# Inverse transforms moved ahead of v's first chunk, four patch-row buffers, and more groups of the 1x1 layer early

## The chip, the cores and the metric

The kernel runs on one core of a Trainium2 chip. The metric is the device time of one execution in microseconds (us). Three runs of the kernel before gave 2798.39, 2808.57 and 2824.54 us, the median being 2808.57 us.

## The reference

The input is x of shape (16, 32, 128, 128) in fp32. Two blocks follow each other, each added to its input:

```python
    x = x + _L0_conv_ref(_gn(x), ...)      # gated depthwise 3x3 with mixed kernels, then 1x1
    x = x + _L1_conv_ref(_gn(x), ...)
```

`_gn` has one channel per group, so it normalises every channel of an image by its own mean and variance. The change lies in the second block, which is

```python
        hidden = jnp.einsum('oc,bchw->bohw', w_hidden, x)          # 32 -> 192 channels
        hidden = lax.conv_general_dilated(hidden, w_dw, ...)       # depthwise 3x3
        q, k, v = jnp.split(hidden, 3, axis=1)                     # 64 channels each
        q_fft = jnp.fft.rfft2(to_patch(q).astype(jnp.float32))     # patches of 8x8
        k_fft = jnp.fft.rfft2(to_patch(k).astype(jnp.float32))
        out = jnp.fft.irfft2(q_fft * k_fft, s=(p, p))
        ...
        mu = out.mean(axis=1, keepdims=True)                       # over the 64 channels
        var = out.var(axis=1, keepdims=True)
        out_norm = (out - mu) / jnp.sqrt(var + 1e-05)
        out_norm = out_norm * norm_w[None, :, None, None] + norm_b[None, :, None, None]
        gated = v * out_norm
        return jnp.einsum('oc,bchw->bohw', w_out, gated)
```

## The kernel before, in words

Stage one (to about 520 us) runs the first block image by image and stores the normalised result to memory with a zero border. Stage two (from about 560 us) runs the second block in 32 **units**, each half an image (64 rows of 128 pixels). Every engine has a written-out list of instructions; semaphores alone tie them together, and each engine runs its list strictly in order. A unit has two parts on every engine.

- **front(u, half, tail)** interleaves two things. For unit u, the 1x1 layer of q and k: VectorE copies a row of patches with their border (`window`, line 1099) into one of the `win` buffers, four groups of matmuls read each (`hidden_group`, line 558; 32 groups in a unit), and ScalarE copies each group's result out of one of three PSUM banks (`windows_out`, line 811). For the unit before (`tail` = u - 1), its end: VectorE takes statistics over the channels of the inverse transform Y (`pixel_stats`, line 1109, and `variance`, lines 1115 and 1117), GpSimd raises them to -1/2 (`roots`, line 441), VectorE centres and scales Y in eight pieces (lines 1122 and 1129), TensorE transposes a piece (`turn`, line 590), ScalarE copies it to `gated` (`turned_out`, line 820), VectorE multiplies it by v (`gate`, line 1134), and TensorE projects two pieces at a time (`project`, line 599); `residual` (line 1141) adds the input. v itself is a dense 3x3 convolution in eight chunks (`v_chunk`, line 577, 18 matmuls each), into three PSUM banks in turn; from chunk 3 on a chunk waits for the gate two chunks back. Groups of the 1x1 layer are spread inside the chunks by a table.
- **spectral(u, ...)** does the transforms of unit u: q's (`q_octet`, line 637) and k's (`k_quad`, line 654, sixteen of them), VectorE's sixteen products of both (line 1199) into the `prod` buffers, and the inverse (`inverse_octet`, line 670, eight of them), whose results ScalarE copies to Y in pairs (`inverse_out`, line 865; `s_y_ready`). The list ends with v's chunk 0 of unit u and, behind it, inverse octets 6 and 7. The statistics of the next front wait for both copies of that last pair.

A gate stands in VectorE's list ahead of the patch-row copy of its turn, and waits for ScalarE's copy of the transposed piece. A patch-row copy waits until the groups that read its buffer last are done. The first two patch rows of a unit are copied in the spectral part before.

## Time and profile before

| what | us |
|---|---|
| median of 3 runs | 2808.57 (2798.39 to 2824.54) |
| the profiled execution, its own time | 2816.34 |
| its span, first to last instruction | 2814.5 |
| TensorE busy | 2513.6 (89%) |
| VectorE busy | 1650.5 (59%) |
| ScalarE busy | 1440.8 (51%) |
| GpSimd busy | 471.8 (17%) |
| TensorE's mean granted clock | 0.965 of full speed |

Busy shares are averages over both stages. The timeline of an engine lists merged runs of instructions with their start, their length and, in brackets, the idle time before them with what ended it. The table of waits sums such idle times by the line that waited and the line that released it. Ends of matmuls are modelled, so the start of the next instruction is the safer mark on TensorE. In the profile fp32 matmuls are recorded twice (16 instructions of line 670 stand as x32).

### The profile page before, as it was taken

Reading aid. Unit: us, or ns where it says so; the run is one execution under the profiler, and the core shown is the slowest. Engines: PE = TensorE matmul, PEld = TensorE weight load, DVE = VectorE, ACT = ScalarE, POOL = GpSimd, SP = SyncE. Lnnn points to the kernel's source line nnn. Section 1 sums busy time; section 2 is a strip of 40 time slices with the busy share of each in tenths; the row PEclk is TensorE's granted clock in tenths of the full one; section 3 lists DMA queues with packets and bytes.
Section 4 is the critical chain, followed back from the end, with each engine's and each line's share of the span. In section 5 each row is a group of like instructions: output and inputs, shape, how many; then the busy total and the mean of one; then the engine's idle time right before and its main releaser. Section 6 shows DMA issues by size and latency. Waiting matters only on the chain.

```text
span 2814.5 us, 90655 instructions
## 1 busy us (share of the span) xinstructions
PE 2513.6 (89%) x40199; PEld 1659.2 (59%) x40199; DVE 1650.5 (59%) x4058; ACT 1440.8 (51%) x2381; POOL 471.8 (17%) x322
## 2 busy tenths in 40 slices
PE   7888889789999999999999899998999989999998
PEld 3333333466666666666666666666666666666665
DVE  4656666455555555555555556555555555656555
ACT  3545555645455555555555455555555555555552
POOL 1000000021111212112121112122212122212221
PEclk9988988899999999999999999999999999999999
DMA  6788887622222222222222222222222222222221
GB/s 128 184 214 202 213 227 203 165 66 62 57 63 59 63 63 67 63 59 67 59 67 63 59 63 63 63 65 61 67 63 66 61 62 66 68 60 67 63 52 46
DMA packets 60345, 248.30 MB, mean 88 GB/s; under 512 B 12393, under 2 KB 12658, under 8 KB 53714
## 3 DMA queue, kind: packets, MB, share of 16 engines
q1 hardware_dynamic: 59954, 242.50, 35.3%
q8 instruction: 317, 5.19, 0.8%
q14 instruction: 74, 0.61, 0.1%
HBM read 140.74 MB, written 101.72 MB: 86 GB/s over the span
## 4 chain that ended last, share of the span: by engine, by line
PE 58%; DVE 14%; ACT 5%; issue 3%; SPq 0%; DMA 0%; DVEq 0%
PE bank L654 16%; PE bank L577 11%; PE bank L670 9%; PE bank L637 7%; PE bank L590 6%; PE bank L558 5%; ACT arena L820 4%; PE bank L599 4%; DVE arena L1109 3%; DVE arena L1122 3%; DVE arena L1134 2%; DVE arena L1129 2%; DVE arena L1099 2%; DVE arena L1141 2%; ACT arena L865 1%
## 5 line engine op out<-in xcount | busy, mean ns | idle before, releaser
L441 POOL TENSOR_TENSOR arena<-arena 128x8 f32<-128x8 f32 x256 | 447.6, 1748 | 1814.8 <-DVE arena L1115 1809.8
L577 PE MATMUL bank<-arena 128*64 128x512 f16 x4608 | 713.4, 403 | 5.5 <-ACT arena L865 5.5
L811 ACT ACTIVATE arena<-bank 100x512 f32<-100x512 f32 x1024 | 615.7, 630 | 183.8 <-PE bank L558 166.7
L1199 DVE TENSOR_TENSOR arena<-bank,arena 128x512 f32<-128x512 f32 x512 | 354.1, 692 | 457.4 <-PE bank L654 370.6
L558 PEld LDWEIGHTS bank<-arena 128*36 128x36 f16 (+1 forms) x8192 | 332.0, 106 | 382.5 <-DVE arena L1099 157.8
L654 PE MATMUL bank<-arena 100*64 100x128 f32 x8192 | 513.1, 274 | 15.4 <-issue 8.7
L558 PE MATMUL bank<-arena 128*36 128x128 f16 (+1 forms) x8192 | 406.1, 224 | 122.1 <-DVE arena L1099 115.8
L654 PEld LDWEIGHTS bank<-arena 100*64 100x64 f32 x8192 | 457.5, 136 | 54.4 <-issue 47.3
L512 PE MATMUL bank<-arena 32*32 32x508 f32 (+1 forms) x9216 | 389.7, 660 | 57.7 <-issue 42.9
L820 ACT ACTIVATE arena<-bank,arena 128x256 f32<-128x256 f32 x512 | 261.1, 560 | 191.6 <-PE bank L590 189.6
L865 ACT ACTIVATE arena<-bank 128x512 f32<-128x512 f32 x256 | 139.1, 596 | 406.1 <-PE bank L670 406.1
L1134 DVE TENSOR_TENSOR arena<-arena,bank 128x512 f32<-128x512 f32 x256 | 176.0, 687 | 270.1 <-ACT arena L820 268.7
L857 ACT ACTIVATE arena<-bank 128x512 f32<-128x512 f32 x256 | 149.2, 598 | 338.6 <-PE bank L637 325.2
L1109 DVE BATCH_NORM_STATS2 arena<-arena 128x6 f32<-128x128 f32 x1024 | 221.9, 279 | 139.2 <-ACT arena L865 139.2
L637 PE MATMUL bank<-arena 100*64 100x128 f32 x4096 | 274.3, 275 | 4.7 <-ACT arena L857 3.2
L512 PEld LDWEIGHTS bank<-arena 32*32 32x32 f32 x9216 | 142.7, 108 | 207.2 <-issue 177.2
L577 PEld LDWEIGHTS bank<-arena 128*64 128x64 f16 x4608 | 211.2, 112 | 87.8 <-ACT arena L865 11.0
L670 PE MATMUL bank<-arena 64*64 64x256 f32 x4096 | 254.8, 383 | 1.3 <-issue 1.3
L637 PEld LDWEIGHTS bank<-arena 100*64 100x64 f32 x4096 | 233.2, 137 | 30.6 <-issue 17.9
L590 PE MATMUL bank<-arena 128*128 128x128 f32 x1024 | 181.9, 301 | 66.6 <-DVE arena L1129 59.9
L590 PEld LDWEIGHTS bank<-arena 128*128 128x128 f32 x1024 | 133.8, 195 | 167.2 <-DVE arena L1129 101.2
L670 PEld LDWEIGHTS bank<-arena 64*64 64x64 f32 x4096 | 143.6, 131 | 84.4 <-issue 32.7
(112 smaller groups left out, 1620.6 us busy)
## 6 DMA issues: line engine op xcount, KB each, us to landing
arena<-xn_d SPq DMA_DIRECT2D x128, 536.2 KB, 8.3
xn_d<-arena SPq DMA_DIRECT2D x130, 260.0 KB, 4.5
x_d<-arena SPq DMA_DIRECT2D x64, 512.0 KB, 8.3
arena<-x_d SPq DMA_DIRECT2D x128, 256.0 KB, 4.9
out<-arena SPq DMA_DIRECT2D x128, 256.0 KB, 5.3
arena<-x_in SPq DMA_DIRECT2D x32, 544.0 KB, 10.1
arena<-x_in SPq DMA_DIRECT2D x32, 528.0 KB, 10.0
arena<-spectra_in SPq DMA_DIRECT2D x1, 1152.0 KB
```

The lines of the kernel that those rows point to most:

```text
L441: pool.tensor_tensor(tiny["rstd"][:, slot], tiny["var_eps"][:, slot], powers, ALU.pow).then_inc(s_root, 1)
L512: mm = pe.matmul(at(psum_of(t, r)[32 * c:32 * c + 32, :], low, [W, 4], [1, high - low]), conv_w[b % 2][32 * r:32 * r + 32, 32 * tap:32 * t ...
L558: mm = pe.matmul(banks[g % ring][low:high, 128 * i:128 * i + 128], w[:, first + low:first + high], hidden_w, start=True, stop=True)
L577: mm = pe.matmul(v_banks[chunk % 3][64 * s:64 * s + 64, :], v_w[:, 64 * tap:64 * tap + 64], at(xs[half], row * WP + 32 * k + dx, [32 * WP, ...
L590: tr = pe.transpose(t_bank[:, 128 * i:128 * i + 128], at(Y, 8 * k + 4 * jr + i, [32, 128]), ident)
L637: mm = pe.matmul(banks[m % 2][64 * par:64 * par + 64, 128 * pair:128 * pair + 128], G_q[0:WIN, 64 * ch:64 * ch + 64], hwin[0:WIN, 128 * ch ...
L654: mm = pe.matmul(k_banks[n % 3][64 * par:64 * par + 64, 256 * part + 128 * pair:256 * part + 128 * pair + 128], G_k[0:WIN, 128 * ch + 64 * ...
L670: mm = pe.matmul(i_banks[par][64 * lam:64 * lam + 64, 256 * (m % 2):256 * (m % 2) + 256], small["inverse"][64 * par:64 * par + 64, 64 * pa ...
L811: act.activation(h_rows[0:WIN, :, first:first + 4], banks[g % ring][0:WIN, :].rearrange("p (i c) -> p c i", i=4), ACT.Copy).then_inc(s_h_r ...
L820: ins = act.activation(at(gated[jr], 256 * lam, [32, 8], [8, 4], [1, 8]), at(banks[4], 64 * lam, [8, 8], [128, 4], [1, 8]), ACT.Identity, ...
L1109: ins = dve.bn_stats(T["pixel_stats"][:, first:first + 6], at(Y, 2048 * s + 4 * p + j, [32, 64], [1, 2]))
L1199: dve.tensor_tensor(parts(prod[m % 4][:, 512 * second:512 * second + 512]), parts(k_banks[n % 3]), q_sb[m % 2][:, 256 * second:256 * secon ...
```

## The change

- **TensorE.** Inverse octets 6 and 7 of a unit now stand ahead of v's chunk 0 instead of behind it. The wait for the last products, which stood ahead of the chunk's last tap, is now ahead of octet 7. Three groups of the 1x1 layer instead of two stand ahead of chunk 1, five instead of four are inside it, and the chunks after it hold 5, 5, 4, 4, 3, 3 instead of 5, 5, 5, 4, 4, 3. ScalarE's list follows (8, 5, 5, 4, 4, 3, 3 groups ahead of the transposed pieces instead of 6, 5, 5, 5, 4, 4, 3).
- **VectorE.** There are four `win` buffers instead of two, so four patch rows instead of two are copied in the spectral part before; the other four come one before the loop over pieces, and three in it, ahead of the gate instead of behind it.
- **Memory.** The `prod` buffers go from four to three to make room.

The first place is **TensorE's list at the seam between two units**: the last k_quads (line 654, 652 in the changed file), v's chunks (577, 575), the inverse (670, 668) and the groups of the 1x1 layer (558). Before:

```order
L670 MATMUL bank<-arena 64x256 x16
L654 MATMUL bank<-arena 64x128 x24
L577 MATMUL bank<-arena 64x512 x18
L670 MATMUL bank<-arena 64x256 x16
L558 MATMUL bank<-arena 64x128
L558 MATMUL bank<-arena 36x128
L558 MATMUL bank<-arena 64x128
...
L558 MATMUL bank<-arena 64x128
L558 MATMUL bank<-arena 36x128
L577 MATMUL bank<-arena 64x512 x6
L558 MATMUL bank<-arena 64x128
L558 MATMUL bank<-arena 36x128
```

The same place now:

```order
L668 MATMUL bank<-arena 64x256 x16
L652 MATMUL bank<-arena 64x128 x24
L668 MATMUL bank<-arena 64x256 x16
L575 MATMUL bank<-arena 64x512 x18
L558 MATMUL bank<-arena 64x128
L558 MATMUL bank<-arena 36x128
L558 MATMUL bank<-arena 64x128
...
L558 MATMUL bank<-arena 64x128
L558 MATMUL bank<-arena 36x128
L575 MATMUL bank<-arena 64x512 x4
L558 MATMUL bank<-arena 64x128
L558 MATMUL bank<-arena 36x128
```

The inverse pair (x16) and chunk 0 (x18) have changed places. The rows left out are groups of the 1x1 layer alone, eight rows a group: two groups before, three now, and then one more inside chunk 1, after its first six matmuls before and after its first four now.

The second place is **VectorE's list from the ninth product of a unit to the second scale of the front**: products (line 1199, 1198 in the changed file), patch-row copies (1099, 1100), centre (1122, 1123) and scale (1129, 1130). Before:

```order
L1199 TENSOR_TENSOR arena<-bank,arena 128x512 x7
L1099 COPY arena<-arena 128x1600
L1199 TENSOR_TENSOR arena<-bank,arena 128x512 x3
L1099 COPY arena<-arena 128x1600
L1199 TENSOR_TENSOR arena<-bank,arena 128x512 x4
...
L1129 TENSOR_TENSOR arena<-arena 128x128x4
L1099 COPY arena<-arena 128x1600
L1122 TENSOR_TENSOR arena<-arena 128x128x4
L1129 TENSOR_TENSOR arena<-arena 128x128x4
L1099 COPY arena<-arena 128x1600
```

The same place now:

```order
L1198 TENSOR_TENSOR arena<-bank,arena 128x512 x7
L1100 COPY arena<-arena 128x1600
L1198 TENSOR_TENSOR arena<-bank,arena 128x512 x2
L1100 COPY arena<-arena 128x1600
L1198 TENSOR_TENSOR arena<-bank,arena 128x512
L1100 COPY arena<-arena 128x1600
L1198 TENSOR_TENSOR arena<-bank,arena 128x512 x2
L1100 COPY arena<-arena 128x1600
L1198 TENSOR_TENSOR arena<-bank,arena 128x512 x2
...
L1130 TENSOR_TENSOR arena<-arena 128x128x4
L1123 TENSOR_TENSOR arena<-arena 128x128x4
L1130 TENSOR_TENSOR arena<-arena 128x128x4
L1100 COPY arena<-arena 128x1600
```

Two more patch-row copies stand among the products, and the copy between the first scale and the second centre is gone.

The third place is **VectorE's list in the front, where the second and third gates stand** (gate 1134, 1135 in the changed file; statistics 1109, 1115, 1117, now 1110, 1116, 1118). Before:

```order
L1109 BN_STATS arena<-arena 128x6 x4
L1115 TENSOR_SCALAR arena<-arena 128x8
L1117 COPY arena<-arena 128x8
L1134 TENSOR_TENSOR arena<-arena,bank 128x512
L1122 TENSOR_TENSOR arena<-arena 128x128x4
L1129 TENSOR_TENSOR arena<-arena 128x128x4
L1099 COPY arena<-arena 128x1600
L1109 BN_STATS arena<-arena 128x6 x4
```

The same place now:

```order
L1110 BN_STATS arena<-arena 128x6 x4
L1116 TENSOR_SCALAR arena<-arena 128x8
L1118 COPY arena<-arena 128x8
L1100 COPY arena<-arena 128x1600
L1135 TENSOR_TENSOR arena<-arena,bank 128x512
L1123 TENSOR_TENSOR arena<-arena 128x128x4
L1130 TENSOR_TENSOR arena<-arena 128x128x4
L1110 BN_STATS arena<-arena 128x6 x4
```

The copy stood behind the gate, centre and scale, and stands ahead of the gate.

The diff:

```diff
--- before.py
+++ after.py
@@ -265,7 +265,7 @@
         hwin = take(128 * 128)
         Y = take(64 * 64)
         q_sb = [take(512) for _ in range(2)]
-        prod = [take(1024) for _ in range(4)]
+        prod = [take(1024) for _ in range(3)]
         gated = [take(512) for _ in range(2)]
         res = take(2048)
         xs_1, xs_0 = [take(HALF * WP, f16) for _ in range(2)]
@@ -273,7 +273,7 @@
         assert stage1_end <= top[0] - (HALF * WP + 1) // 2
         G_q = take(64 * 64)
         G_k = take(64 * 128)
-        win = [take(1632, f16) for _ in range(2)]
+        win = [take(1632, f16) for _ in range(4)]
 
 
         block = ctx.enter_context(nc.Block())
@@ -416,11 +416,11 @@
             pool.wait_ge(s_prep_v, 1)
             pool.memset(xh.bitcast(f32), 0.0).then_inc(s_pads_zero, 1)
             pool.memset(xl.bitcast(f32), 0.0).then_inc(s_pads_zero, 1)
-            for s in range(2):
+            for s in range(4):
                 pool.memset(win[s][:, 16 * WIN:1632].bitcast(f32), 0.0).then_inc(s_win_room, 1)
             pool.wait_ge(s_pool_consts, 2)
             pool.wait_ge(s_pads_zero, 2)
-            pool.wait_ge(s_win_room, 2)
+            pool.wait_ge(s_win_room, 4)
 
             for b in range(-1, NB + 1):
                 pool.wait_ge(s_ve, b + 2)
@@ -551,7 +551,7 @@
                     pe.wait_ge(s_x2_ready, NCH * NB)
                 if positive(32 * u + g + 1 - ring):
                     pe.wait_ge(s_h_ready, 32 * u + g + 1 - ring)
-                w = win[g // 4 % 2]
+                w = win[g // 4 % 4]
                 for i in range(4):
                     first = (4 * (g % 4) + i) * WIN
                     for low, high in ((0, 64), (64, WIN)):
@@ -559,7 +559,7 @@
                                        start=True, stop=True)
                 mm.then_inc(s_hidden_mm, 1)
 
-            def v_chunk(u, half, k, jr, groups, between, before_last=None):
+            def v_chunk(u, half, k, jr, groups, between):
 
                 chunk = 2 * k + jr
                 if chunk == 0:
@@ -569,8 +569,6 @@
                 if chunk > 2:
                     pe.wait_ge(s_gated, 8 * u + chunk - 2)
                 for tap in range(9):
-                    if tap == 8 and before_last is not None:
-                        before_last()
                     dy, dx = tap // 3, tap % 3
                     for s in range(2):
                         row = 8 * (2 * s + jr) + dy
@@ -615,14 +613,14 @@
                     hidden(16)
                     return
                 v_half = 1 - half
-                hidden(2)
+                hidden(3)
                 for k in range(4):
-                    v_chunk(tail, v_half, k, 1, (4, 5, 4, 3)[k], hidden)
+                    v_chunk(tail, v_half, k, 1, (5, 5, 4, 3)[k], hidden)
                     if k > 0:
                         project(tail, k - 1)
                     turn(tail, k, 0)
                     if k < 3:
-                        v_chunk(tail, v_half, k + 1, 0, (5, 5, 4)[k], hidden)
+                        v_chunk(tail, v_half, k + 1, 0, (5, 4, 3)[k], hidden)
                     if k < 3 or u is None:
                         turn(tail, k, 1)
 
@@ -669,7 +667,7 @@
                             for lam in range(2):
                                 mm = pe.matmul(i_banks[par][64 * lam:64 * lam + 64, 256 * (m % 2):256 * (m % 2) + 256],
                                                small["inverse"][64 * par:64 * par + 64, 64 * part:64 * part + 64],
-                                               at(prod[m % 4][64 * par:64 * par + 64, :], 256 * part + 64 * lam, [512, 2], [128, 2], [1, 64]),
+                                               at(prod[m % 3][64 * par:64 * par + 64, :], 256 * part + 64 * lam, [512, 2], [128, 2], [1, 64]),
                                                start=part == 0, stop=part == 1)
                     mm.then_inc(s_inverse_mm, 1)
 
@@ -689,9 +687,12 @@
                     k_quad(2 * m + 1)
                     if m == 0 and tail is not None:
                         project(tail, 3)
-                v_chunk(u, half, 0, 0, 0, None, lambda: inverse_inputs(7))
+                pe.wait_ge(s_prod_ready, 16 * u + 14)
+                pe.wait_ge(s_y_ready, 8 * u + 6)
                 inverse_octet(6)
+                pe.wait_ge(s_prod_ready, 16 * u + 16)
                 inverse_octet(7)
+                v_chunk(u, half, 0, 0, 0, None)
 
             front(0, 0, None)
             spectral(0, 0, None)
@@ -841,7 +842,7 @@
                     high(NB - 1, 1)
                     act.wait_ge(s_xl_ready, 4 * NB)
                     return
-                for p, groups_before in enumerate((6, 5, 5, 5, 4, 4, 3)):
+                for p, groups_before in enumerate((8, 5, 5, 4, 4, 3, 3)):
                     some(groups_before)
                     turned_out(tail, p // 2, p % 2)
                 if u is None:
@@ -1092,11 +1093,11 @@
 
             def window(u, half, r, b=None):
 
-                if positive(32 * u + 4 * (r - 1)):
-                    dve.wait_ge(s_hidden_mm, 32 * u + 4 * (r - 1))
+                if positive(32 * u + 4 * (r - 3)):
+                    dve.wait_ge(s_hidden_mm, 32 * u + 4 * (r - 3))
                 if r == 0:
                     dve.wait_ge(s_xs_in[half], 64 * (b + 1))
-                dve.tensor_copy(win[r % 2][:, 0:16 * WIN].rearrange("p (j y x) -> p j y x", y=10, x=10),
+                dve.tensor_copy(win[r % 4][:, 0:16 * WIN].rearrange("p (j y x) -> p j y x", y=10, x=10),
                                      at(xs[half], 8 * r * WP, [8, 16], [WP, 10], [1, 10])).then_inc(s_win_ready, 1)
 
             def pixel_stats(u, p):
@@ -1141,7 +1142,7 @@
                 dve.tensor_tensor(piece, banks[6].rearrange("p (l r w) -> p l r w", l=2, r=8), piece, ALU.add).then_inc(s_res_done, 1)
 
             def front(u, half, tail):
-                rows = iter(range(2, 8) if u is not None else ())
+                rows = iter(range(4, 8) if u is not None else ())
 
                 def windows(n=1):
                     for r in islice(rows, n):
@@ -1150,7 +1151,6 @@
                 if tail is None:
                     second_stats(NB - 1, range(4, NCH))
                     aggregate(NB + 2, NB - 1, None)
-                    windows(2)
                     quarter_variance(NB + 2, None)
                     low(NB - 2, 0)
                     low(NB - 2, 1)
@@ -1168,7 +1168,6 @@
                     if p == 1:
                         centre(tail, 0)
                 scale(tail, 0)
-                windows()
                 centre(tail, 1)
                 scale(tail, 1)
                 windows()
@@ -1176,6 +1175,8 @@
                     if p < 5:
                         pixel_stats(tail, p + 3)
                         variance(tail, p + 3)
+                    if p > 0:
+                        windows()
                     if p < 7 or u is None:
                         gate(tail, p // 2, p % 2)
                     if p < 6:
@@ -1183,8 +1184,6 @@
                         scale(tail, p + 2)
                     if p in (2, 4, 6):
                         residual(tail, p // 2 - 1)
-                    if p > 0:
-                        windows()
 
             def spectral(u, tail, nxt):
                 if tail is not None:
@@ -1193,20 +1192,20 @@
                     m, second = n // 2, n % 2
                     dve.wait_ge(s_q_copied, 8 * u + m + 1)
                     dve.wait_ge(s_k_mm, 16 * u + n + 1)
-                    if positive(8 * u + m - 3):
-                        dve.wait_ge(s_inverse_mm, 8 * u + m - 3)
+                    if positive(8 * u + m - 2):
+                        dve.wait_ge(s_inverse_mm, 8 * u + m - 2)
                     parts = lambda a: a.rearrange("p (part x) -> p part x", part=2)
-                    dve.tensor_tensor(parts(prod[m % 4][:, 512 * second:512 * second + 512]), parts(k_banks[n % 3]),
+                    dve.tensor_tensor(parts(prod[m % 3][:, 512 * second:512 * second + 512]), parts(k_banks[n % 3]),
                                       q_sb[m % 2][:, 256 * second:256 * second + 256].unsqueeze(1).broadcast_to([128, 2, 256]),
                                       ALU.mult).then_inc(s_prod_ready, 1)
                     if n == 1 and tail is not None:
                         residual(tail, 3)
-                    if nxt is not None and n in (8, 11):
-                        window(nxt[0], nxt[1], (n - 8) // 3, nxt[2])
-
-            dve.wait_ge(s_win_room, 2)
-            window(0, 0, 0, 0)
-            window(0, 0, 1, 0)
+                    if nxt is not None and n in (8, 10, 11, 13):
+                        window(nxt[0], nxt[1], (8, 10, 11, 13).index(n), nxt[2])
+
+            dve.wait_ge(s_win_room, 4)
+            for r in range(4):
+                window(0, 0, r, 0)
             front(0, 0, None)
             dve.wait_ge(s_xn_out, 128 * NB)
             spectral(0, None, (1, 1, 0))
```

## Rows read from the trace of the kernel before

**Rows 1.** The page, the chain that ended last: share of the span by engine.

```profile
PE 58%; DVE 14%; ACT 5%; issue 3%; SPq 0%; DMA 0%; DVEq 0%
```

**Rows 2.** Waits of TensorE, 590 to 2790 us: total us, times, longest us.

```profile
PE bank L558 <- DVE arena L1099: 111.5, 93, 1.6
PE bank L590 <- DVE arena L1129: 59.9, 32, 2.7
PE bank L654 <- issue: 8.7, 6, 1.8
```

**Rows 3.** Timeline of TensorE, one unit: start us, length us, instructions, idle before.

```profile
1015.01 2.23 PE L577 MATMUL bank<-arena 128*64 128x512 f16 x18
1017.17 1.98 PE L670 MATMUL bank<-arena 64*64 64x256 f32 x32
1019.08 0.64 PE L558 MATMUL bank<-arena 128*64 128x128 f16 x16
...
1024.86 0.71 PE L590 MATMUL bank<-arena 128*128 128x128 f32 x4 [1.85 <-DVE arena L1129]
...
1031.04 0.65 PE L577 MATMUL bank<-arena 128*64 128x512 f16 x4
...
1034.23 1.02 PE L599 MATMUL bank<-arena 128*64 128x512 f32 x4
...
1038.59 0.39 PE L577 MATMUL bank<-arena 128*64 128x512 f16 x2
1040.22 0.41 PE L558 MATMUL bank<-arena 128*64 128x128 f16 x8 [1.25 <-DVE arena L1099]
```

**Rows 4.** Timeline of VectorE, same unit, same columns.

```profile
1015.28 0.69 DVE L1199 TENSOR_TENSOR arena<-bank,arena 128x512 f32<-128x512 f32 x1 [0.18 <-PE bank L654]
1020.34 0.88 DVE L1109 BATCH_NORM_STATS2 arena<-arena 128x6 f32<-128x128 f32 x4 [4.36 <-ACT arena L865]
...
1024.11 0.69 DVE L1129 TENSOR_TENSOR arena<-arena 128x512 f32<-128x512 f32 x1
...
1031.57 0.87 DVE L1109 BATCH_NORM_STATS2 arena<-arena 128x6 f32<-128x128 f32 x4
...
1032.62 0.68 DVE L1134 TENSOR_TENSOR arena<-arena,bank 128x512 f32<-128x512 f32 x1
1033.22 0.69 DVE L1122 TENSOR_TENSOR arena<-arena 128x512 f32<-128x512 f32 x1
1034.01 0.69 DVE L1129 TENSOR_TENSOR arena<-arena 128x512 f32<-128x512 f32 x1
1034.62 0.57 DVE L1099 COPY arena<-arena 128x1600 f16<-128x1600 f16 x1
```

**Rows 5.** Timeline of ScalarE, same unit.

```profile
1019.22 1.09 ACT L865 ACTIVATE arena<-bank 128x512 f32<-128x512 f32 x2 [5.65 <-PE bank L670]
...
1025.61 1.02 ACT L820 ACTIVATE arena<-bank,arena 128x256 f32<-128x256 f32 x2 [1.94 <-PE bank L590]
...
1032.06 3.05 ACT L811 ACTIVATE arena<-bank 100x512 f32<-100x512 f32 x5
```

**Rows 6.** Timeline of GpSimd, same unit.

```profile
1021.57 5.82 POOL L441 TENSOR_TENSOR arena<-arena 128x8 f32<-128x8 f32 x3 [44.48 <-DVE arena L1115]
1029.73 1.64 POOL L441 TENSOR_TENSOR arena<-arena 128x8 f32<-128x8 f32 x1 [2.35 <-DVE arena L1115]
```

**Rows 7.** Timeline of TensorE: v's chunk 0 (units 0, 30, 31), last first transpose.

```profile
591.14 2.23 PE L577 MATMUL bank<-arena 128*64 128x512 f16 x18
...
2700.25 2.23 PE L577 MATMUL bank<-arena 128*64 128x512 f16 x18
...
2769.27 2.24 PE L577 MATMUL bank<-arena 128*64 128x512 f16 x18
...
2779.12 0.71 PE L590 MATMUL bank<-arena 128*128 128x128 f32 x4 [2.73 <-DVE arena L1129]
```

**Rows 8.** Stretches: us, busy PE, PEld, DVE, ACT, POOL, granted clock, DMA share, GB/s.

```profile
1025.50:1029.60 4.10, 4.10 (x41) 2.53 (x42) 2.62 (x10) 2.55 (x5) 1.88 (x1) 0.58 0.01 4
```

## The prediction

> **What bounds the kernel now.** I read the chain of waits by engine first: 58% of the span is TensorE, 14% VectorE, 5% ScalarE [rows 1]. So the question is where TensorE stands still. The table of TensorE's waits answers it for stage two: 111.5 us in groups of the 1x1 layer that wait for a patch-row copy, 59.9 us in transposes that wait for VectorE's scale, and 8.7 us in k_quads that wait for nothing the profile shows [rows 2]. Then I laid the timelines of one unit side by side and measured on TensorE from start to start.
>
> Times from here on are in us after the first matmul of v's chunk 0, which stands at 1015.01 [rows 3]. *Before*: chunk 0 runs 0 to 2.16, the inverse pair 2.16 to 4.07, and then the groups begin [rows 3]. ScalarE's two Y copies start 2.05 after the pair does and last 1.09; VectorE starts its statistics at 5.33 and ends the first scale 4.46 later, at 9.79 [rows 4, 5]; the first transpose starts at 9.85 [rows 3]. TensorE has by then run two groups and a chunk with four. A chunk alone is 2.16 and a chunk with five groups 3.19 (1031.04 to 1034.23), so a group is some 0.21 [rows 3]. Its work ends near 4.07 + 0.42 + 3.04 = 7.6. It stands for about 2.2, of which the profile books 1.85 at the transpose and the rest, with modelled ends, elsewhere.
>
> The group waits have one pattern. The gate stands ahead of the patch-row copy in VectorE's list, the gate waits for ScalarE's copy of a transposed piece, and the next groups wait for the patch row. Such a stall is longer than it is booked: at 1038.59 two matmuls of a chunk start, worth 0.24, and the group behind them starts at 1040.22, so 1.39 against 1.25 [rows 3].
>
> **The change, part by part.**
>
> *Inverse ahead of chunk 0.* Octet 6 needs products that are long done. Octet 7 needs the product of the sixteenth k_quad: 0.27 to 0.96 [rows 4]. Octet 6 takes half of the pair's 1.91 us and ends at 0.96. With 0.06 from VectorE's end to TensorE's start (first scale to transpose, 1024.80 to 1024.86 [rows 3, 4]) octet 7 starts at 1.05: a new stall of 0.1. The pair ends at 2.0, ScalarE copies from 2.15 to 3.24, statistics start at 3.27, and the first scale ends at 7.73, so the transpose may start at 7.8. The same copies of Y are now hidden behind chunk 0.
>
> *TensorE up to there.* 2.0, chunk 0 to 4.2, three groups to 4.8, chunk 1 with five groups to 8.0 or 8.1. Work ends after the data are there: no stall, 0.3 to spare. Three banks take the groups' results. ScalarE needs 0.61 a group (3.05 for five [rows 5]), and its first starts about 4.7, so the fourth group (5.3) meets a bank that comes free at 5.3. Inside a chunk a group comes every 0.7, slower than ScalarE. Cost here: 0 to 0.2, taken as nothing.
>
> The transpose starts at 8.1 instead of 9.85 with two more groups done: 1.75 + 0.42 = **2.2 us a unit**.
>
> *Four patch-row buffers, copies ahead of the gates.* VectorE's spacing in the front is 1.05 for statistics, 0.60 gate, 0.79 centre, 0.61 scale, about 0.5 copy [rows 4]. Carried on from 7.73: second scale to 9.1, the fifth patch row to 9.6, statistics to 10.6, first gate 10.6 to 11.3, the sixth row at 14.2, the seventh at 17.8, the eighth at 22.9. TensorE, without a stall, wants these rows at 15.3, 19.8, 23.6 and 28. Each is there 5 us early, so none of the three stalls is left: 111.5 / 31 = 3.6 a unit booked, and 0.15 more for each of three, **4.0 us a unit**.
>
> *What is late next.* The gates. TensorE's own walk has transposes at 8.1, 12.0, 16.9, 20.6, 25.1, 28.6 and 33.0. From a transpose ScalarE starts after 0.75 and takes 1.02 [rows 3, 5], then the gate 0.69. Chunk 3 starts at 12.7 and wants the first gate (11.3). The projections start at 15.9, 24.2 and 32.0 and want the second, fourth and sixth gate (14.95, 23.6, 31.2). Nothing is late, the least margin is 0.6.
>
> *Two more copies among the products.* The one behind the fourteenth product holds back the fifteenth by 0.2 and ends before the sixteenth can start; the one behind the eleventh holds back the twelfth by 0.2, which TensorE wants 0.4 later still. Three `prod` buffers: each product waits for an inverse three octets back, and that stands ahead of the k_quad it needs in TensorE's list. Both cost nothing; if their cover were gone they cost 0.2 to 0.5 a unit. The start of stage two waits for memory, and is as before.
>
> *The clock.* In the stretch behind the 1.85 us idle time TensorE's granted clock is 0.58 on average, mostly the lower level of 1.2 GHz [rows 8]. Not all units have it. The last unit's period is 69.02 (2700.25 to 2769.27), the mean of 31 is (2769.27 - 591.14) / 31 = 70.26 [rows 7]. So 31 x 1.24 = 38.4 us lie above the undisturbed unit; 8.7 are the waits for nothing [rows 2], **29.7** I put on the clock. What came before the fall was a TensorE that stood still. With the stall gone I expect all of it back; bounds 0 and 29.7, and I take the upper one, since in no other place of the unit does it fall.
>
> For the waits for nothing the Trainium skill has "Runtime: NRT & Kernel Launch", section "Instruction fetch mechanics": instructions are fetched in blocks while the engine runs on, and crossing a block is "mostly hidden". If these waits are fetches, the trace disagrees in six places of up to 1.8 us [rows 2]; by that rule they would be nearly gone and the time 8.7 lower. I leave them where they are.
>
> *The end.* Behind the last unit there are no groups. Its first transpose waits for the same chain: 9.85 now (2769.27 to 2779.12 [rows 7]), 7.8 after: **2.1**.
>
> Sum: 31 x (2.2 + 4.0) = 192, and 29.7, and 2.1: 224 us. From the profiled execution's own 2816.3 that is **2592 us**. The median of the runs shown is 0.3% lower, at 2808.6; I hold that the runs differ mostly in how many units have the low clock, which is gone afterwards, so I leave it at 2592.
>
> **The rivals.**
>
> *The clock falls all the same.* For it: the small matmuls of the groups are more crowded near the first transpose, and I have only one cause by timing. Price: 29.7 back, 2622. Chance 13%.
>
> *The first transpose waits, or the gates do, for GpSimd.* It needs 5.82 for its first three roots where one alone takes 1.64 [rows 6], and the second root ends just when the second scale wants it (8.4). VectorE is now denser there. If the second scale comes up to 1.4 later, so do the first two gates, and the first projection waits up to 0.3 to 1: 10 to 31 us, 2602 to 2623. Against it: a single root beside three tensor operations of VectorE still took 1.64. Chance 8%. The Trainium skill speaks for this rival in "SBUF — State Buffer": VectorE and GpSimd share a port pair as an exclusive lock that an instruction holds to its end. The first three roots (1.94 each) agree in direction, the single one does not show it.
>
> *The copies are not what the groups wait for.* Then ScalarE's banks would be, at once, and the 4.0 would shrink to half: 2654. Against it: no wait of a group for ScalarE stands in the table. Chance 4%.
>
> *A denser TensorE is granted less clock through the whole front.* This is the one that ends slower. Price: work at 0.58 takes 1.72 times as long, so once 9 us of each front's 33 run low, the 6.2 gained are lost; were it half of a front, 31 x (12 - 6.2) = +180, 2996. Against it: the spectral part is dense now and no part of it is known to fall; a clock that falls behind busy time was not seen. Chance 2%. Some 2% more are for the change not coming to effect, 2800.
>
> **How the numbers follow.** My forecast has 71%. It holds from 2575 (8.7 of the waits go, and some noise: the runs before spread by 0.9%) to 2610 (0.1 to 0.5 a unit in small stalls at the banks). The range reaches to the clock and GpSimd rivals: 2572 to 2640. Two executions of this kernel cannot be told apart by much less than 1%. Faster by over 1%: 0.95; within 1%: 0.02; slower by over 1%: 0.03.
>
> **What would show it.** The waits of a group for a patch row near 0 instead of 111.5; the wait of the transpose for the scale near 0; a wait of octet 7 for a product of about 0.1 a unit; a unit's period near 62.8; a granted clock near 1 in every front. The forecast is wrong if the transpose still waits over 0.5 a unit, if groups wait for ScalarE's copies, or if the low clock stays with no idle time ahead of it.

## The result and the profile after

The changed kernel takes 2586.6 us (median of 4 runs, 2583.2 to 2590.4) against 2807.2 us before (4 runs); the ratio is 0.921, 95% interval 0.916 to 0.925. The forecast was 2592 us, from 2572 to 2640. The profiled execution took 2588.67 us with a span of 2586.9, against 2816.34 and 2814.5.

The chain of waits of the changed kernel, by engine, answers to [rows 1]. In the profile after, line numbers are shifted: 575 is v's chunk, 588 the transpose, 597 the projection, 635 q, 652 k, 668 the inverse, 812 and 821 ScalarE's copies, 866 its Y copies, 1100 the patch rows, 1110 the statistics, 1130 the scale, 1135 the gate, 1142 the residual, 1198 the products.

```profile
PE 76%; issue 1%; ACT 1%; DVE 0%; SPq 0%; DMA 0%; ACTq 0%
```

VectorE's 14% are gone from it, and TensorE is busy 95% of the span. The waits of TensorE in stage two, 560 to 2560 us (total, times, longest), answer to [rows 2]:

```profile
PE bank L652 <- issue: 7.0, 6, 1.6
PE bank L652 <- DVE arena L1198: 6.7, 1, 6.7
PE bank L588 <- ACT arena L821: 5.5, 31, 0.2
PE bank L588 <- DVE arena L1130: 1.5, 1, 1.5
```

The 111.5 us of groups that waited for a patch row have no row any more. Of the transposes' 59.9 us one wait of 1.5 is left, in the last front, which has no groups. The 6.7 stand once, at the start of stage two. One unit on TensorE (start, length, instructions), for [rows 3]; the point zero of the prediction, the end of the last k_quad, is now the start of the inverse pair:

```profile
966.38 2.84 PE L652 MATMUL bank<-arena 100*64 100x128 f32 x48
969.15 2.02 PE L668 MATMUL bank<-arena 64*64 64x256 f32 x32
971.11 2.25 PE L575 MATMUL bank<-arena 128*64 128x512 f16 x18
973.20 0.83 PE L558 MATMUL bank<-arena 128*64 128x128 f16 x24
...
977.14 0.71 PE L588 MATMUL bank<-arena 128*128 128x128 f32 x4
...
1002.64 1.10 PE L635 MATMUL bank<-arena 100*64 100x128 f32 x16
```

The pair takes 1.96 from start to start (1.91 in [rows 3]), so octet 7's wait for its product costs 0.05. The first transpose comes 7.99 after the last k_quad instead of 9.85, with two more groups done, and no row of the front has an idle time in brackets. VectorE and ScalarE at the same seam, for [rows 4, 5]; first VectorE:

```profile
968.19 0.57 DVE L1100 COPY arena<-arena 128x1600 f16<-128x1600 f16 x1
968.67 1.35 DVE L1198 TENSOR_TENSOR arena<-bank,arena 128x512 f32<-128x512 f32 x2
972.36 0.87 DVE L1110 BATCH_NORM_STATS2 arena<-arena 128x6 f32<-128x128 f32 x4 [2.34 <-ACT arena L866]
...
976.14 0.69 DVE L1130 TENSOR_TENSOR arena<-arena 128x512 f32<-128x512 f32 x1
...
982.76 0.57 DVE L1100 COPY arena<-arena 128x1600 f16<-128x1600 f16 x1
983.25 0.68 DVE L1135 TENSOR_TENSOR arena<-arena,bank 128x512 f32<-128x512 f32 x1
```

ScalarE's Y copies:

```profile
971.24 1.08 ACT L866 ACTIVATE arena<-bank 128x512 f32<-128x512 f32 x2 [3.64 <-PE bank L668]
```

The new patch-row copy at 968.19 sits in front of the last two products and they follow it back to back; they end at 970.02, 0.87 after the last k_quad (0.96 before). The Y copies start 2.09 after it, the statistics 3.21, the first scale ends at 7.68. The copy at 982.76 now stands ahead of the gate at 983.25, which finds its data.

The inverse pair of units 0, 30 and 31, and the last front's first transpose, for [rows 7]:

```profile
589.86 2.02 PE L668 MATMUL bank<-arena 64*64 64x256 f32 x32
...
2482.86 2.02 PE L668 MATMUL bank<-arena 64*64 64x256 f32 x32
...
2545.50 2.02 PE L668 MATMUL bank<-arena 64*64 64x256 f32 x32
...
2553.23 0.71 PE L588 MATMUL bank<-arena 128*128 128x128 f32 x4 [1.46 <-DVE arena L1130]
```

An undisturbed unit now lasts 62.64 (69.02 before) and the mean of 31 is (2545.50 - 589.86) / 31 = 63.09 (70.26 before). An undisturbed unit is the shortest kind, with no wait for nothing and a full clock. In these terms the 227.6 us between the two spans are 31 x 6.38 = 197.8 in the undisturbed unit, 24.7 in what disturbs units (38.5 before, 13.8 now), 1.3 before the first of them and 3.8 behind the last. The granted clock over a whole front (columns as in [rows 8]) is full:

```profile
964.40:1002.60 38.20, 38.20 (x556) 23.97 (x552) 28.70 (x81) 27.07 (x49) 14.16 (x8) 1.00 0.04 8
```

### The profile page after: what moved, and what is told of

The parts are those of the page before. It is cut to its first block, busy times and chain, and to the rows that moved or that the text cites. A ratio compares the mean times of both kernels' runs of the same rounds, so it can differ in the third digit from the quotient of the medians.

```text
span 2586.9 us, 90657 instructions
## 1 busy us (share of the span) xinstructions
PE 2465.4 (95%) x40199; PEld 1644.8 (64%) x40199; DVE 1638.6 (63%) x4058; ACT 1432.4 (55%) x2381; POOL 476.5 (18%) x324
## 3 DMA queue, kind: packets, MB, share of 16 engines
q1 hardware_dynamic: 59954, 242.50, 38.5%
## 4 chain that ended last, share of the span: by engine, by line
PE 76%; issue 1%; ACT 1%; DVE 0%; SPq 0%; DMA 0%; ACTq 0%
PE bank L575 21%; PE bank L652 18%; PE bank L668 10%; PE bank L558 9%; PE bank L635 8%; PE bank L588 6%; PE bank L597 4%; ACT arena L821 1%; SPq L318 0%; DMA xn_d<-arena 0%; DVE arena L1110 0%; DVE arena L961 0%; ACT arena L866 0%; DVE arena L1198 0%; DVE arena L1135 0%
## 5 line engine op out<-in xcount | busy, mean ns | idle before, releaser
L575 PE MATMUL bank<-arena 128*64 128x512 f16 x4608 | 689.3, 393 | 0.0
L812 ACT ACTIVATE arena<-bank 100x512 f32<-100x512 f32 x1024 | 604.2, 628 | 95.8 <-PE bank L558 74.4
L558 PE MATMUL bank<-arena 128*36 128x128 f16 (+1 forms) x8192 | 388.9, 220 | 11.0 <-DVE arena L1100 4.2
L575 PEld LDWEIGHTS bank<-arena 128*64 128x64 f16 x4608 | 205.6, 109 | 96.3 <-issue 12.4
L1130 DVE TENSOR_TENSOR arena<-arena 128x512 f32<-128x512 f32 x256 | 178.3, 696 | 23.4
```

The source lines that it names most:

```text
L558: mm = pe.matmul(banks[g % ring][low:high, 128 * i:128 * i + 128], w[:, first + low:first + high], hidden_w, start=True, stop=True)
L575: mm = pe.matmul(v_banks[chunk % 3][64 * s:64 * s + 64, :], v_w[:, 64 * tap:64 * tap + 64], at(xs[half], row * WP + 32 * k + dx, [32 * WP, ...
L812: act.activation(h_rows[0:WIN, :, first:first + 4], banks[g % ring][0:WIN, :].rearrange("p (i c) -> p c i", i=4), ACT.Copy).then_inc(s_h_r ...
```

## The experiments

Ratios are against the kernel before, on the same chip. "Booked" is idle time as a profile writes it. Sums of waits are over all of stage two, from the first unit's end of the k_quads to the last front, unless another stretch is named.

### The two halves apart

**Patch rows alone** (four buffers, four copies in the spectral part, copies ahead of the gates):

```diff
-        win = [take(1632, f16) for _ in range(2)]
+        win = [take(1632, f16) for _ in range(4)]
...
-        prod = [take(1024) for _ in range(4)]
+        prod = [take(1024) for _ in range(3)]
...
-                    if nxt is not None and n in (8, 11):
+                    if nxt is not None and n in (8, 10, 11, 13):
...
+                    if p > 0:
+                        windows()
                     if p < 7 or u is None:
                         gate(tail, p // 2, p % 2)
...
-                    if p > 0:
-                        windows()
```

> The kernel before with the four patch-row buffers, the four copies in the spectral part and the copies ahead of the gates alone; inverse pair, group tables as before. Theory (two separate stalls, and a clock that falls behind the transpose's stall): the three group stalls go, 31 x 4.0 = 124 us, the transpose still waits about 1.8 us booked in every unit and the low clock stays in about half of the units: about 2683 us. Rival (the clock falls because of the group stalls): the low clock goes too, about 2655. Rival (the groups really wait for ScalarE's banks): half of the gain, about 2745.

Measured: 2662 us, ratio 0.950 (0.946 to 0.953). The waits of TensorE:

```profile
PE bank L590 <- DVE arena L1129: 59.9, 32, 2.7
PE bank L654 <- issue: 8.4, 6, 1.8
```

The group stalls are gone and the transpose's stall is untouched, as the theory has it, but the time is 21 us under it, near the rival's. An undisturbed unit is 64.86, so the group stalls were 4.16 a unit (69.02 before). I took a unit as low in clock where its period less its booked idle time lies over 1 us above the least of its kernel, in the units from one end of the k_quads to the next, the first of 31 left out: 15 of 30 before, 4 of 30 here. The granted clock over a unit picks out the same ones: 0.97 to 0.98 in these, 1.00 in the others. So most of the low clock went although the stall that stands ahead of it stayed.

**Inverse pair ahead of chunk 0, and the new group tables:**

```diff
-                hidden(2)
+                hidden(3)
...
-                    v_chunk(tail, v_half, k, 1, (4, 5, 4, 3)[k], hidden)
+                    v_chunk(tail, v_half, k, 1, (5, 5, 4, 3)[k], hidden)
...
-                        v_chunk(tail, v_half, k + 1, 0, (5, 5, 4)[k], hidden)
+                        v_chunk(tail, v_half, k + 1, 0, (5, 4, 3)[k], hidden)
...
-                v_chunk(u, half, 0, 0, 0, None, lambda: inverse_inputs(7))
+                pe.wait_ge(s_prod_ready, 16 * u + 14)
+                pe.wait_ge(s_y_ready, 8 * u + 6)
                 inverse_octet(6)
+                pe.wait_ge(s_prod_ready, 16 * u + 16)
                 inverse_octet(7)
+                v_chunk(u, half, 0, 0, 0, None)
...
-                for p, groups_before in enumerate((6, 5, 5, 5, 4, 4, 3)):
+                for p, groups_before in enumerate((8, 5, 5, 4, 4, 3, 3)):
```

> The kernel before with the inverse pair ahead of chunk 0 and the new group tables; two patch-row buffers, copies behind the gates. Theory: the transpose's stall goes (31 x 2.2 + 2 = 70 us) and with it the low clock (25 to 30): about 2710 us, the three group stalls as before, 3.6 us a unit. Rival (clock tied to the group stalls): 2737 with the low clock still in half of the units. Rival (the two parts need each other, since groups that come earlier wait longer for their patch rows): the group stalls grow by what the transpose gives, under 20 us gained.

Measured: 2845 us, ratio 1.014 (1.011 to 1.018): slower than before. Of the three only the last mechanism is near, and it is worse than I had it: the group waits are 200.9 us, in 124 waits of up to 2.5. No unit waits for the scale at the transpose any more (the one wait left, 1.4, is in the last front), and yet 20 of 30 are low in clock. So the transpose's stall is not needed for the low clock. The next two runs take the slowdown apart.

**Inverse pair alone** (of that diff the lines around the two octets):

> The kernel before with the inverse pair ahead of chunk 0 alone. Theory: the transpose can start 2.05 us earlier (7.8 after the point where the last k_quad ends) and TensorE's work ends at 7.65, so the booked wait falls from 1.85 to under 0.3: 31 x 2.0 + 2 = 64 us, and the low clock 25 to 30: about 2716 us. Rival (the groups ahead are what covers the chain): the wait stays over 0.5 a unit and the time over 2740.

Measured: 2721 us, ratio 0.971 (0.966 to 0.975). As expected: no wait for the scale is left in the units, group waits are 112.2 us (93 waits, as before), and no unit of 30 is low in clock.

**Group tables alone** (the other lines; 3 groups, then 5, 5, 5, 4, 4, 3, 3):

> The kernel before with the new group tables alone (3, then 5, 5, 5, 4, 4, 3, 3). Theory: the transpose starts when its data are there, 9.85 us after the last k_quad, whatever TensorE does before it; two groups of 0.21 us fill the wait: 31 x 0.4 = 13 us, booked wait about 1.4 instead of 1.85, perhaps some of the low clock: 2780 to 2794. Rival (more work ahead is as good as an earlier inverse): over 40 us gained.

Measured: 2911 us, ratio 1.039 (1.035 to 1.043). Both expectations fall. The waits of TensorE, with the same columns:

```profile
PE bank L558 <- DVE arena L1099: 207.6, 123, 2.5
PE bank L590 <- DVE arena L1129: 36.2, 32, 2.7
PE bank L558 <- ACT arena L811: 11.1, 31, 0.4
```

The transposes wait 23.7 us less: 1.08 booked in a unit instead of 1.85, of which the two groups fill 0.4 and another 0.35 is now booked at ScalarE's banks. But the groups wait 96 us more, four times in an undisturbed unit (1.72, 2.15, 1.56, 1.70) instead of three. And 21 of 30 units are low in clock. On TensorE one of these stalls:

```profile
1060.56 0.71 PE L590 MATMUL bank<-arena 128*128 128x128 f32 x4
...
1062.82 0.62 PE L577 MATMUL bank<-arena 128*64 128x512 f16 x4
1065.59 0.41 PE L558 MATMUL bank<-arena 128*64 128x128 f16 x8 [2.15 <-DVE arena L1099]
```

and on VectorE at the same time:

```profile
1062.36 0.69 DVE L1134 TENSOR_TENSOR arena<-arena,bank 128x512 f32<-128x512 f32 x1 [2.45 <-ACT arena L820]
1062.97 0.69 DVE L1122 TENSOR_TENSOR arena<-arena 128x512 f32<-128x512 f32 x1
1063.76 0.69 DVE L1129 TENSOR_TENSOR arena<-arena 128x512 f32<-128x512 f32 x1
1064.37 0.68 DVE L1141 TENSOR_TENSOR arena<-bank,arena 128x512 f32<-128x512 f32 x1
1064.97 0.57 DVE L1099 COPY arena<-arena 128x1600 f16<-128x1600 f16 x1
```

The transpose at 1060.56 has to go through ScalarE and the gate before VectorE comes to the patch row. With the old table the first group of that row stood far enough behind the transpose; one or two groups earlier in the list it stands right behind it, and the whole way of 4.4 us from transpose to patch row is on TensorE's path, less what a part of a chunk covers. Behind this stall the granted clock falls too (1066 to 1070):

```profile
1066.00:1070.00 4.00, 4.00 (x35) 2.32 (x32) 1.34 (x6) 2.38 (x5) 1.64 (x1) 0.57 0.00 0
```

### Place or number of buffers

**Copies ahead of the gates alone**, two buffers, old tables, pair behind chunk 0:

```diff
+                    if p > 0:
+                        windows()
                     if p < 7 or u is None:
                         gate(tail, p // 2, p % 2)
...
-                    if p > 0:
-                        windows()
```

> The kernel before with the copies ahead of the gates alone: two buffers, old tables, inverse pair behind chunk 0. Theory: the copy that waits behind gate, centre and scale comes 2 us earlier and no longer behind ScalarE's copy, so the three group stalls go without any more buffer: about 2662 us, as the kernel with four buffers and copies ahead of the gates. Rival (two buffers hold the copy back, because it waits for the groups that read the buffer): less than half of that, over 2740.

Measured: 2681 us (2663 to 2681; the profile is of the 2663), ratio 0.953 (0.949 to 0.957), beside 0.950 for the run with four buffers: intervals that overlap. The group waits are gone (the transposes' 60.0 us stay). Moving the two lines gives nearly all of the group term without a buffer, but not quite: an undisturbed unit is 65.18, 0.32 more than with four buffers. It stands at the first projection, which lasts 1.35 us (1248.66) instead of 1.02, since its second half waits for the second gate; ahead of that gate VectorE has one patch-row copy more to do in the front, and waits 0.40 for its buffer (1242.71 to 1243.11). The profile books none of this on TensorE.

**New tables and copies ahead of the gates**, two buffers, pair behind chunk 0:

> The kernel before with the new group tables and the copies ahead of the gates: two buffers, inverse pair behind chunk 0. The new tables alone cost 104 us, with group stalls of 1.7 and 2.2 us. Theory (the tables ask for the fourth and fifth patch rows one gate earlier, and only a copy that stands behind that gate is late): ahead of the gates the stalls go, and the tables fill part of the transpose's wait: 2645 to 2665 us. Rival (two buffers are too few for the new tables): group stalls of 1 us or more in every unit, over 2700.

Measured: 2649 us, ratio 0.944 (0.941 to 0.946). This is as the theory has it. The same tables that cost 104 us with the copies behind the gates gain some 24 with the copies ahead (31 x 0.79: an undisturbed unit is 64.39, against 65.18 in the run before this one). The waits of groups for patch rows are gone, the transposes of the units wait 33.4 us in all, and 11.1 us are waits for ScalarE's banks, 0.4 each.

**The changed kernel with the copies behind the gates**, four buffers:

```diff
-                    if p > 0:
-                        windows()
                     if p < 7 or u is None:
                         gate(tail, p // 2, p % 2)
...
+                    if p > 0:
+                        windows()
```

> The changed kernel with the patch-row copies of the front behind the gates, as they stood before (four buffers stay). Theory: with four buffers the copies have 1.6 to 3.4 us to spare even behind the gates (sixth row ready at 16.4 for 19.8, seventh at 22.0 for 23.6, eighth at 25.5 for 28), so nothing waits: 2587 us, as the changed kernel. Rival (the place ahead of the gate is what counts): group waits come back, some 1 us a unit, 2620.

Measured: 2585 us, ratio 0.921 (0.917 to 0.924). No difference, and no group wait.

**The changed kernel with two patch-row buffers** (and four product buffers), copies ahead of the gates:

> The changed kernel with two patch-row buffers and four product buffers: inverse pair ahead of chunk 0, new tables, copies ahead of the gates. Theory (order alone is enough): rows 4 to 7 ready at 14.7, 18.3, 22.4, 26.5 for groups that want them at 15.3, 19.8, 23.6, 28: 2587 to 2600 us. Rival (with the new tables the groups run ahead of two buffers, as in the runs with the tables alone, whatever stands ahead of the gate): 1 us a unit or more, over 2620.

Measured: 2588 us, ratio 0.922 (0.919 to 0.925). No difference either: an undisturbed unit is 62.63 us in all three. Buffers and place are two cures for one stall, and in this kernel either is enough.

**The changed kernel with the old group tables:**

> The changed kernel with the group tables of before (2, then 4, 5, 5, 5, 4, 4, 3). Theory: TensorE has the same work and its transpose waits 0.15 us at most: 2587 to 2592 us, so the tables are worth nothing where the inverse pair stands ahead. Rival (the tables cover the chain): a wait of 0.4 us or more in every unit, over 2600.

Measured: 2599 us, ratio 0.926 (0.922 to 0.929); an undisturbed unit is 62.83. This lies between the two expectations, so neither is right in size. TensorE's rows there:

```profile
971.07 2.02 PE L668 MATMUL bank<-arena 64*64 64x256 f32 x32
...
978.29 0.39 PE L558 MATMUL bank<-arena 128*64 128x128 f16 x8
978.80 0.71 PE L588 MATMUL bank<-arena 128*128 128x128 f32 x4
```

The transpose stands 7.73 behind the last k_quad, 0.05 after the scale has ended (978.75), and 0.51 behind the last group, where it stands 0.32 behind it when nothing is awaited (976.82 to 977.14 in the changed kernel). The stall of 0.2 is hidden in a matmul's modelled end and booked as nothing; 31 of them are 6 us of the 12.

### The clock, and the start of stage two

**A long stall at the transpose and nowhere else.** The changed kernel, the first scale held back until GpSimd's third root:

```diff
+                dve.wait_ge(s_root, 8 * tail + 3)
                 scale(tail, 0)
                 centre(tail, 1)
```

> The changed kernel with the first scale of each front held back until GpSimd's third root is done, 2.8 us later than in the changed kernel, so that TensorE waits some 2.4 us (booked 2.2) at the first transpose of every unit and nowhere else. Theory (the low clock needs the transpose's stall together with the group stalls, since with either alone it was nearly gone): 31 x 2.4 = 74 us more, the clock stays high in nearly all units: 2655 to 2670 us. Rival (a single stall of over 2 us is enough for the clock): low clock in half of the units or more, 1.6 us each, 2685 to 2720.

Measured: 2682 us, ratio 0.957 (0.954 to 0.959), with booked waits of 2.2 in every unit. The time lies between theory and rival, and the clock is low in 7 of 30 units (the first one, left out, is an eighth). In one of them the fall stands right behind the stall (1190 to 1194 us):

```profile
1190.00:1194.00 4.00, 3.78 (x30) 2.38 (x32) 3.86 (x12) 1.64 (x3) 0.81 (x1) 0.57 0.02 4
```

In the run with the patch rows alone, one of the four low units has it elsewhere, behind a wait for nothing of 1.56 us in the spectral part (836 to 840 us):

```profile
836.00:840.00 4.00, 3.57 (x34) 1.92 (x33) 0.69 (x1) 0.00 (x0) 0.00 (x0) 0.62 0.38 151
```

The other three of that run have it behind the transpose's 1.85, and six of the seven of the other behind the transpose's 2.2. So a stall of 1.5 to 2.2 us can be followed by the low clock without any group stall, and mostly is not: "both stalls together" is refuted as a condition. Nine of these eleven low units also had a wait for nothing of 0.6 to 1.7 us, two of them right ahead of the fall, the others 28 to 31 us ahead of it. But of the 15 low units of the kernel before only four had one, so that is no condition either.

The low clock does not need a stall that the change removes. The changed kernel with the copies behind the gates has it in one unit of 30, right behind a wait for nothing:

```profile
1770.34 0.45 PE L652 MATMUL bank<-arena 100*64 100x128 f32 x4 [1.88 <-issue]
...
1770.00:1774.00 4.00, 3.66 (x36) 2.02 (x36) 0.69 (x1) 0.00 (x0) 0.00 (x0) 0.58 0.37 140
```

The next run below has it in two of 30, behind such waits of 1.6 and 2.0 us. What decides between one unit and the next stays open.

**No wait for the stores at the start of stage two:**

```diff
-            dve.wait_ge(s_xn_out, 128 * NB)
             spectral(0, None, (1, 1, 0))
```

> The changed kernel without VectorE's wait, ahead of the first product of stage two, for all stores of the normalised images. With three product buffers those buffers no longer share memory with the tile that is being stored; the wait is for nothing. In the changed kernel TensorE stands 6.7 us in the third k_quad there and VectorE 10.3 us for the stores. Theory: the products begin some 9 us earlier, the ninth product's patch-row copy then waits some 2 us for its load, 6 to 9 us gained: 2578 to 2581 us. Rival (the load of the next half's rows, which waits for the same stores, sets the pace): the wait moves there, under 2 us gained.

**The changed kernel again, on the same chip:**

> The changed kernel as it is, beside the next one on the same chip. Theory and rival alike: 2587 us, from 2580 to 2592.

Measured: 2586.8 us without the wait (0.922, 0.920 to 0.925), 2585.7 with it (0.922, 0.920 to 0.924): nothing gained, the rival. VectorE's rows there:

```profile
570.84 0.69 DVE L1198 TENSOR_TENSOR arena<-bank,arena 128x512 f32<-128x512 f32 x1 [1.05 <-PE bank L652]
578.43 0.58 DVE L1100 COPY arena<-arena 128x1600 f16<-128x1600 f16 x1 [6.90 <-DMA arena<-xn_d]
```

VectorE gets through nine products, and then the patch-row copy waits 6.9 us for its load, which waits for the same stores. The wait has moved down the list. No version here beats the changed kernel by what can be measured.

## Why the prediction was right, step by step

- **Inverse ahead of chunk 0: right.** Octet 7's stall 0.05 (0.1 forecast), statistics at 3.21 (3.27), first scale's end 7.68 (7.73), the transpose at 7.99 (8.1). The pair alone gained 86 us: 2.0 a unit (67.02 against 69.02), the rest mostly the clock.
- **The group stalls: right in size, and the walk held.** Patch rows alone gave 4.16 a unit (4.0 forecast). Both terms together were forecast as 6.2 a unit; measured 6.38. That the stalls were longer than booked was the point that mattered: 5.6 of booked idle time went from an undisturbed unit (5.77 before, 0.18 now). The transposes behind the first come at 11.9, 16.7, 20.4, 25.0, 28.5 and 32.9 (12.0, 16.9, 20.6, 25.1, 28.6 and 33.0 forecast). The prediction gave the term to four buffers and the move ahead of the gates as one edit. In the changed kernel each alone gives it.
- **The tables: valued right only where they stand.** I counted them as 0.42 a unit of filling. In the changed kernel they are worth 0.2 a unit. With the kernel before around them they cost 104 us, which no sentence of the prediction saw, since it walked the whole change at once.
- **The clock: the size near, the cause wrong.** I tied the low clock to the transpose's stall alone, because no other place of the unit showed it. The patch rows alone leave that stall as it was, and the low clock shrinks from 15 units to 4; inverse pair and tables together leave no such stall, and 20 units are low. The step failed in its cause and came out right partly by luck, since the change removes all of the unit's booked stalls but one of 0.18. The size was 24.7 us in all that disturbs units, where 29.7 were forecast for the clock. The 29.7 held too much: of the 13.8 us by which the units of the changed kernel still lie above the undisturbed one, at full clock in every unit, 8.2 are waits for nothing and 5.6 are small delays that are not booked.
- **GpSimd: no wait for it.** Three first roots took 5.34 us (5.82 before), later single ones up to 1.90. Nothing waited for them.
- **Waits for nothing:** seven of them with the one of the inverse, 8.2 us, against seven and 10.0 before (of which I left the 8.7 of the k_quads in). They did not go, as the rule on instruction fetch in "Runtime: NRT & Kernel Launch" of the Trainium skill (section "Instruction fetch mechanics") would have had it, if they are fetches. The trace says more of them than I used. The page of the profile has a DMA queue of instructions, 16 KB a packet (queue and kind, packets, MB, share of 16 engines):

```profile
q8 instruction: 317, 5.19, 0.9%
```

  One of its packets starts 2.6 to 3.0 us before TensorE goes on in each of the seven waits, and its 1.2 to 1.4 us end 1.3 to 1.7 us before that point. The same holds for the seven of the kernel before. In stage two such a packet comes once in 8 to 9 us, so fourteen of fourteen are hardly chance: the waits look like instruction fetches. No run changed the fetches, so that is not shown by an experiment.
- **The end:** the last first transpose at 7.73 behind the last k_quad, 7.8 forecast. The end as a whole gave 3.8 instead of 2.1. In the kernel before, the chunk behind that transpose took 3.60 us at a granted clock of 0.58, and takes 2.26 now. The prediction had put no low clock there.
- **The slower rival:** a dense TensorE was granted the full clock through the whole front.

## What to carry to other kernels

In a list that an engine runs in order, an operation without a data dependence still inherits every wait ahead of it. Look for the cheap copy that feeds the bound engine behind an operation that waits for a round trip over two other engines; moving it ahead and giving it buffers cured the same stall here, and moving costs no memory. Measure stalls from start to start where ends are modelled, and do not take a table that was set for one order of the lists over to another untested: this one gained 12 us in one order and cost 104 in another.

## What the runs showed of the hardware

- The mean granted clock of TensorE was 0.57 to 0.62 over some 4 us (the lower level, 1.2 GHz, for most of it) behind stalls of 1.5 to 2.2 us, but not behind each. Low units of 30: 15 with a stall of 1.85 and three of 0.9 to 1.5; 20 with group stalls of 1.0 to 2.2 and none at the transpose; 4 with 1.85 alone and 7 with 2.2 alone; none with 1.25, 0.9 and 1.5 alone. In the changed kernel it was none, and in two variants of it one and two, behind waits for nothing of 1.6 to 2.0.
- TensorE's waits without a visible cause, 0.45 to 1.8 us, each came with a 16 KB packet of the instruction queue that had started 2.6 to 3.0 us before the engine went on (14 of 14 in the kernels before and after).
- A single root on GpSimd, with the same operands, took 1.64 us, and 1.90 where VectorE's fp16 patch-row copy ran as it started (982.76 beside the root at 982.92). That is so for 93 of the 160 single roots of the changed kernel, and for one with the copies behind the gates.
